# Transposes, values and the output's evacuation three heads behind the scores instead of two, with the same buffers

## The reference

```python
xn = layernorm(x)                                  # x: 32 x 512 x 256
# attention with relative positions, 16 heads of 16
content_score = einsum('bhsp,bhtp->bhst', q + u, k)
pos_score     = relative_shift(einsum('bhsp,htp->bhst', q + v, pos))
weights = softmax((content_score + pos_score) / sqrt(16))
att = einsum('bhst,bhtp->bhsp', weights, val)      # then @ Wo + bo
# mixture of 8 experts, over the same tokens: softmax gate, top k per expert,
# gelu(xin @ w1) @ w2, weighted, added back to the chosen rows
x = x + att_out + ffn_out
```

## Time and profile before

| | us |
|---|---|
| median of three runs | 4815.69 |
| lowest and highest | 4812.66, 4815.70 |
| the profiled execution | 4826.3 |
| its span in the profile | 4824.4 |
| TensorE busy | 4458.8 |
| VectorE busy | 3669.3 |
| ScalarE busy | 3441.5 |
| GpSimd busy | 1710.0 |

### The profile page before, as it was taken

The page is one execution under the profiler, slowest core; times in us unless marked ns, Lnnn a source line. Parts: engine busy times, 40 slices in busy tenths (PEclk is TensorE's granted clock), DMA queues, the critical chain, the costliest instruction groups (busy, mean ns, idle before and its releaser), DMA issues. The chain is left out here.

```text
span 4824.4 us, 127659 instructions
## 1 busy us (share of the span) xinstructions
PE 4458.8 (92%) x50604; PEld 3425.4 (71%) x50604; DVE 3669.3 (76%) x8040; ACT 3441.5 (71%) x5180; POOL 1710.0 (35%) x1545
## 2 busy tenths in 40 slices
PE   7799998989999999999999989879999999999997
PEld 3466666666666666666666666669999999999997
DVE  7699999999999999999999998954554545534344
ACT  3699999999899999999898999844333434344454
POOL 0222322222232232222323222234565656544443
PEclk9899999999999999999999999989999999999999
DMA  9899999999999999999999999973555545433259
GB/s 341 334 368 377 379 374 376 376 372 378 373 383 378 378 382 375 377 377 377 372 373 379 373 372 374 365 249 65 119 135 118 146 108 145 96 63 84 48 158 316
DMA packets 394088, 1390.59 MB, mean 288 GB/s; under 512 B 51104, under 2 KB 128800, under 8 KB 327712
## 3 DMA queue, kind: packets, MB, share of 16 engines
q1 hardware_dynamic: 270624, 778.39, 44.5%
q0 software_dynamic: 122880, 604.05, 38.3%
HBM read 708.00 MB, written 674.23 MB: 287 GB/s over the span
## 5 line engine op out<-in xcount | busy, mean ns | idle before, releaser
L604 ACT ACTIVATE att_shifted<-att_shifted,att_mn 128x512 f32<-128x512 f32 x2048 | 1362.2, 719 | 0.2 <-DVE att_mn L740 0.2
L740 DVE CUSTOM_DVE_ANT_0 att_shifted<-att_quad,att_shifted 128x512 f32<-128x512 f32 x2048 | 1324.2, 683 | 50.1 <-PE att_quad L984 41.7
L599 ACT ACTIVATE ring<-att_quad 128x1024 f32<-128x1024 f32 x1024 | 1049.3, 1025 | 207.0 <-PE att_quad L972 204.7
L750 DVE COPY att_pt<-att_tp 128x512 f32<-128x512 f32 x1536 | 1009.8, 685 | 157.1 <-PE att_tp L1010 142.9
L490 POOL DMA_DIRECT2D att_shifted<-xs_d x512 | 279.3, 546 | 2102.5 <-DMA xs_d<-ring 1817.1
L1472 DVE TENSOR_TENSOR ffn_hp<-ring,ffn_hp 128x512 fp32r<-128x512 f32 x512 | 477.5, 933 | 686.6 <-ACT ring L1409 646.5
L1009 PEld LDWEIGHTS att_tp<-ident,att_shifted 64*128 64x128 f32 x8192 | 597.3, 140 | 517.1 <-ACT att_shifted L604 393.3
L1407 ACT ACTIVATE ffn_hp<-ffn_up 128x512 fp32r<-128x512 f32 x512 | 305.9, 597 | 915.6 <-PE ffn_up L1553 905.8
L1009 PE MATMUL att_tp<-ident,att_shifted 64*128 64x64 f32 x8192 | 727.7, 229 | 204.4 <-DVE att_pt L750 197.9
L972 PE MATMUL att_quad<-att_pos,att_qv 64*128 64x512 f32 x2048 | 870.0, 445 | 15.8 <-ACT ring L599 15.6
L984 PE MATMUL att_quad<-att_kd,att_qu 64*128 64x512 f32 x2048 | 826.7, 451 | 50.8 <-DVE att_mn L740 39.6
(11 more groups left out here) (113 smaller groups left out, 5312.2 us busy)
## 6 DMA issues: line engine op xcount, KB each, us to landing
xs_d<-ring SPq DMA_DIRECT2D x1024, 513.0 KB, 8.9
att_shifted<-xs_d POOLq DMA_DIRECT2D x512, 1024.0 KB, 9.6
att_shifted<-in_L_attn_x_dram SPq DMA_DIRECT2D x32, 512.0 KB, 7.2
xn_d<-att_shifted SPq DMA_DIRECT2D x32, 512.0 KB, 6.3
xt_d<-att_shifted SPq DMA_DIRECT2D x32, 512.0 KB, 7.4
gathered<-xt_d SPq DMA_DIRECT2D x32, 512.0 KB, 12.1
att_d<-att_osb SPq DMA_DIRECT2D x512, 32.0 KB
ring<-in_L_ffn_w_dram SPq DMA_DIRECT2D x16, 1024.0 KB
```

What stands on the lines that cost most here:

```text
L599: act.activation(xo[:, kk % NW, 2 * half:2 * half + 2, 1:S + 1], xp[:, :, :], ACT.Copy).then_inc(x_out, 1)
L604: act.activation(shifted[:, kk % NX, t], shifted[:, kk % NX, t], ACT.Exp, bias=mn[:, kk % NX, t:t + 1], scale=-1.0).then_inc(exp_done, 1)
L740: dve.tensor_tensor_reduce(out=shifted[:, kk % NX, t], in0=sp_[:, t % 2], in1=shifted[:, kk % NX, t], scale=-0.25, scalar=-NEG, op0=ALU.ad ...
L750: dve.tensor_copy(turned_to(t // 2, t % 2), tp[:, t % 2]).then_inc(t_out_dve, 1)
```

## The change

`LAG` becomes 3, and the evacuation of the output moves with it, so that it still comes right behind the fourth head of `op`. Everything that is written with `LAG` follows: the transposes of head kk-3 and the values of head kk-4 stand in step kk, the first steps have none of them for one step more, and what is left after the loop is one head longer. No buffer changes.

```diff
-    LAG = 2
+    LAG = 3
...
                         if not (first and kk < LAG):
                             t_evacuate(i, kk - LAG)
-                        if kk % QH == 2 and not (first and kk < QH):
+                        if kk % QH == LAG and not (first and kk < QH):
                             o_evacuate(i, kk // QH - 1)
```

## The result

The changed kernel takes 4821.84 us (median of 19 executions, 4814.22 to 4832.33) against 4812.66 us (19 executions, 4804.79 to 4818.45) before. The ratio is 1.002, 95% interval 1.0014 to 1.0026: 9.2 us slower (6.7 to 12.5). The profiled execution took 4832.33 us.

What follows compares the result with a forecast made beforehand. A cycle between VectorE and TensorE was taken to set each step, with transfers close beside it. Terms -1.5 + 3 + 5.1 + 0.5 - 2 = +5.1 us on the median 4815.7 gave 4821; range 4797 to 4848.

Steps and rivals of the forecast that it cites:

- L1009's wait is not one for the exponentials: Weight loads of the transposes: the 269.1 us of idle time put down to exponentials is no wait for them.
- Rival A: The weight loads' wait on exponentials is real: faster, 4637 us, or 4688 as the transfers allow; chance 0.03.
- (1): Transposes and values one step later: steady steps keep the same instructions in the same places; 0 us.
- (2): Slots of `shifted`: freed one step later, still four steps, 23 us, ahead of the addition; cost 0.
- (3): Output's evacuation L620 moves from steps 2 and 6 of eight to 3 and 7; -1.5 us (-3 to +31).
- (4): SP's queue: output stores start 0.7 us later, delaying the writes and read behind them; +3 us, 0 to 45.
- laid against each head's slack, 18 would make VectorE wait: Slips of up to 0.65 us in SyncE's queue: 18 exceed their head's slack, 5.2 us of VectorE waits together.
- Rival C: Late stores in SyncE's queue make reads late, at the upper price: slower, 4864 us; chance 0.25.
- (5): Drain: one more head, +5.1 us (2.6 to 5.3); first drained head's values wait for L620, +0.5 (0 to 1.2).
- (6): Start of the phase: third step loses its transposes, fourth its values; -2 us, from -3.7 to 0.
- Rival B: ScalarE's load is spread better: a third to two thirds of 46 us disturbances gone, 4788 to 4803; chance 0.12.

Runs made afterwards that it cites:

- caught up to one: Kernel before (lag two), but a second head is turned in step 28 of the last batch pair, so it ends at lag one; ratio 1.0002.
- the first chip's two runs: Changed kernel with stores and xt loads a step later, 4822.17 us; changed kernel turning a second head in step 28, ending at lag two, ratio 1.001.
- the two kernels with late weights: Kernel before and changed kernel, each with feed-forward weight loads and gathers issued only after the last scores; ratios 0.9999 and 1.0008.

## Why the prediction was right, by its own steps

The direction held, and so did the mechanism as far as the profiles show it: of the 9.2 us, 7.4 are seen at the end of the phase, and no other place shows a loss that is the change's. The sum of +5.1 us was short of the measured 9.2 (6.7 to 12.5). That the forecast of 4821 meets the measured 4821.84 is luck: the kernel before came out 3 us lower over 19 executions (4812.66) than over the first three, and terms that did not come, +3 and -1.5, partly cancel in the sum.

*L1009's wait is not one for the exponentials*: right. 261.0 us after against 269.1, and lag one shows what a real one looks like. Rival A fell with it.

*(1) and (2), steady steps and slots, 0*: right. The mean over the 16 kinds of step of their medians is 5.697 us before and 5.699 after, and from head 16 to 496 lag two took 2782.8 (before) and 2763.0 us (caught up to one), lag three 2776.8 (the change), 2775.3 and 2771.9 (the first chip's two runs). Lag four shows no wait for slots either.

*(3) L620, -1.5*: the medians of the steps with `keep_keys` and of those with `keep_queries` did not move. 0 fits as well; the term can't be seen.

*(4) SyncE's stores, +3 (0 to 45)*: wrong in size for this change. The stores do start later as worked out, 1.16 us after the L599 instead of 0.39, but VectorE's waits on reads went from 10 to 2 in the whole phase, and undoing the move gave nothing back that can be seen. The step that failed is "laid against each head's slack, 18 would make VectorE wait". The mechanism is real one step earlier in the queue, and dearer than the bound I gave it (42 to 60 us), but by the timeline it goes through GpSimd's splits behind the read, and VectorE's late reads are 0 and 1 in the two kernels that lose most. I had put those down at no cost because the slots are free. Rival C was right that such a loss exists and wrong about this change.

*(5) The end, +5.1 and +0.5*: right in kind, mis-sized. The last two pairs are 4.99 us apart. The first drained head comes 5.59 us after the last addition instead of 4.12, 1.5 us more, outside my 0 to 1.2: head 508's values, now behind the loop, wait for the last step's L620 (3156.30), and the transposes of the next head stand behind them. TensorE's row at 3156.99 has that wait, 1.22 us. With the 0.3 that the middle interval is longer, the drain is 6.6 us longer than before; it is 4.6 us longer in the run with the stores a step later, and 5.8 between the two kernels with late weights. The two runs differ by the clock as well: with the stores a step later the third head is drained in 4.3 us at a granted clock of 1.00, in the changed kernel in 4.99 at 0.81. My bound of 2.6 for a drained head at twice the speed was far off, since at the full clock it is 4.28. This is the term that makes the change slower.

*(6) The start, -2*: mis-sized. From head 0's first addition to head 5's, seven lag-two profiles take 29.6 to 31.7 us, 30.9 in the mean, and five lag-three profiles 30.2 to 30.9, 30.4 in the mean: -0.5.

So the sum with measured terms, (1) to (4) at 0, is -0.5 + 6.6 = +6.1 us, just below the interval of the medians' difference (6.7 to 12.5). The whole end grew by 7.4 us in the profiles, which is inside it; the 2 to 3 us up to the medians' 9.2 are not explained. Rival B, +0.09 us of disturbances a head to be won, did not come: the mean interval from head 16 to head 496 went from 5.797 to 5.785 us.

## What to carry to other kernels

A software pipeline pays for each stage of distance once, in its drain (here 5.2 us a head); once the distance covers the producer's latency (here at lag two, where lag one costs 493 us), more of it bought nothing. Before a wait that a trace puts down to a producer is attacked, look at the matmul beside the weight load: here only the load carried the name, and the wait ended on something else. And an issue moved by one step in a DMA queue is to be priced by what stands behind its neighbours on every in-order engine: which of sixteen steps it stood in decided between 0 and 60 us.

## What had not been expected of the hardware

The xt load of 0.5 MB, one step earlier, costs 58 us in 30 places (1.9 us each), although the transfers' total is unchanged. The one wait on the path that has a DMA's name is GpSimd's, and it grew by 3 us inside a total that did not grow.

The granted clock falls ahead of the idle stretch of TensorE, not behind it, in the changed kernel: it is 1.00 from 3108 to 3124 us, where TensorE is busy for 14.15 of 16 us, and 0.50, the lower of its two levels (1.2 GHz), from 3125 to 3165. In the kernel before it is 1.00 from 3125 to 3138 and 0.50 from 3139 to 3159, and from 3150 to 3180 both have 0.61. So both drains are run mostly at the lower level (0.67 before, 0.63 after).

Three of the four chips took 34 to 42 us more for the kernel before than the first one; a lag-two profile of the second has 19 late reads in the phase, the kernel before in its own profile 10.
